# Decoder block: causal self-attention in six units of 512 score columns per row instead of eight

## What is computed

```python
def _L0_attn_ref(hidden_states, Wq, Wk, Wv, Wo):      # H=32, HKV=8, HD=16, S=128
    q = (hidden_states @ Wq.T).reshape(B, Sq, H, HD).transpose(0, 2, 1, 3)
    ...
    k = jnp.repeat(k, rep, axis=1)
    qr = apply_rope(q, cos, sin)
    kr = apply_rope(k, cos, sin)
    ...
    mask = jnp.where(causal_future[None, None, :, :], neg, mask)
    scores = jnp.einsum('bhqd,bhkd->bhqk', qr, kr) / np.sqrt(HD).astype(np.float32) + mask
    attn = jax.nn.softmax(scores, axis=-1)
    out = jnp.einsum('bhqk,bhkd->bhqd', attn, v)
    return out.transpose(0, 2, 1, 3).reshape(B, Sq, Dm) @ Wo.T
...
    x = x + _L0_attn_ref(_layernorm(x, axis=-1), ...)
    x = x + _L0_xattn_ref(_layernorm(x, axis=-1), ctx_4096, ...)
    x = x + _L0_ffn_ref(_layernorm(x, axis=-1), ...)
```

## Time and profile before

| | us |
|---|---|
| median of 3 runs | 1021.59 |
| lowest and highest | 1020.73, 1023.36 |
| the profiled execution | 1023.87 |
| its span | 1021.9 |
| TensorE busy | 951.2 (93%) |
| VectorE busy | 767.4 (75%) |
| ScalarE busy | 607.0 (59%) |
| GpSimd busy | 579.7 (57%) |

### The profile page before, as it was taken

The page is one execution under the profiler, slowest core; times in us unless marked ns, Lnnn a source line. Parts: engine busy times, 40 slices in busy tenths (PEclk is TensorE's granted clock), DMA queues, the critical chain, the costliest instruction groups (busy, mean ns, idle before and its releaser), DMA issues.

```text
span 1021.9 us, 17975 instructions
## 1 busy us (share of the span) xinstructions
PE 951.2 (93%) x5523; PEld 810.7 (79%) x5540; DVE 767.4 (75%) x1603; ACT 607.0 (59%) x2218; POOL 579.7 (57%) x586
## 2 busy tenths in 40 slices
PE   5888888876999999999999999999999999999977
PEld 4666666654888888888888888888888888888766
DVE  5788888775577777777777777777777777788965
ACT  1566666652585576567566755765676666656531
POOL 4443333203486568557656856765685676558743
PEclk9799999987999999999999999999999999999999
DMA  5000002000666646655665665556566555654531
GB/s 196 12 11 11 10 10 72 11 1 0 216 215 211 211 154 226 211 172 165 209 204 175 206 215 170 177 192 217 171 207 204 176 176 191 198 178 149 162 111 54
DMA packets 101138, 149.71 MB, mean 147 GB/s; under 512 B 11840, under 2 KB 77376, under 8 KB 98880
## 3 DMA queue, kind: packets, MB, share of 16 engines
q1 hardware_dynamic: 101056, 148.71, 45.8%
HBM read 87.85 MB, written 60.82 MB: 145 GB/s over the span
## 4 chain that ended last, share of the span: by engine, by line
PE 67%; DVE 4%; ACT 1%; POOL 1%; issue 1%; DMA 1%; SPq 0%; DVEq 0%; POOLq 0%
PE ps_kv L76 17%; PE ps_y L76 17%; PE ps_q L76 16%; PE ps_o L76 8%; PE ps_s L76 8%; ACT ps_s L1034 1%; DVE p L1146 1%; PE ps_f L76 1%; DVE neg_max L1134 1%; POOL pT_raw L952 0%; DVE p_blocks L1150 0%; DVE raw_wkv L1213 0%; DMA out<-raw_wq 0%; DVE kT_lo L1173 0%; DVE f_stats L1203 0%
## 5 line engine op out<-in xcount | busy, mean ns | idle before, releaser
L1034 ACT ACTIVATE ps_s<-ps_s,bias,q_rms 128x256 f32<-128x256 f32 x256 | 136.9, 535 | 139.6 <-DVE bias L1138 139.6
L945 POOL TENSOR_TENSOR qT_lo<-qk_raw,qT_hi 128x512 fp32r<-128x512 f32 x64 | 84.5, 1320 | 202.8 <-ACT qT_hi L1063 202.8
L952 POOL TENSOR_TENSOR pT_raw<-pT_raw,pT_hi_sb 128x1024 fp32r<-128x1024 f32 x64 | 154.4, 2412 | 11.8 <-ACT pT_hi_sb L1057 11.5
L1051 ACT ACTIVATE q_squares<-ps_q 128x128 bf16<-128x128 f32 x256 | 67.4, 278 | 112.1 <-DVE qk_blocks L1168 112.1
L76 PE MATMUL ps_y<-wo_hi,oT_hi 128*128 128x512 f32 x256 | 101.7, 397 | 4.9 <-DVE oT_lo L1184 4.9
L76 PE MATMUL ps_q<-wq_lo,xT_hi 128*128 128x512 f32 x256 | 101.4, 396 | 0.0
L76 PE MATMUL ps_q<-wq_hi,xT_lo 128*128 128x512 f32 x256 | 101.1, 395 | 0.0
L76 PE MATMUL ps_y<-wo_lo,oT_hi 128*128 128x512 f32 x256 | 101.1, 395 | 0.0
L1150 DVE STREAM_TRANSPOSE p_blocks<-p 128x512 f32<-128x512 f32 x128 | 91.1, 711 | 13.3
L76 PE MATMUL ps_q<-wq_hi,xT_hi 128*128 128x512 f32 x256 | 100.9, 394 | 0.0
L76 PE MATMUL ps_y<-wo_hi,oT_lo 128*128 128x512 f32 x256 | 100.9, 394 | 0.0
(11 more groups left out here) (205 smaller groups left out, 3027.6 us busy)
## 6 DMA issues: line engine op xcount, KB each, us to landing
p_scratch<-p_blocks SPq DMA_DIRECT2D x64, 512.0 KB, 3.0
pT_raw<-p_scratch SPq DMA_DIRECT2D x256, 128.0 KB, 3.0
qk_scratch<-qk_blocks SPq DMA_DIRECT2D x64, 384.0 KB, 3.5
qk_raw<-qk_scratch SPq DMA_DIRECT2D x256, 96.0 KB, 3.0
raw_wq<-in_x_wq SPq DMA_DIRECT2D x8, 1024.0 KB, 6.9
raw_wo<-in_x_wo SPq DMA_DIRECT2D x8, 1024.0 KB, 7.2
raw_wkv<-in_x_wkv SPq DMA_DIRECT2D x8, 512.0 KB, 5.0
ctx_raw<-in_ctxT SPq DMA_DIRECT2D x8, 256.0 KB, 2.5
```

The source lines that it names most:

```text
L945: pool.tensor_tensor(qT[1][:].rearrange("p g (i c) -> p g i c", i=4), qk_raw[s % 2][:, :, 0:XG, :].rearrange("p i g c -> p g i c"), f32(qT ...
L952: pool.tensor_tensor(raw, f32(raw), f32(pT_hi_sb[:].rearrange("p i t x -> p (i t x)")), ALU.subtract).then_inc(pT_lo, 1)
L1034: e = act.activation(scores, scores, ACT.Exp, bias=bias[:, g:g + 1], scale=q_rms[:, s % 4, g:g + 1], accum_out=total[:, g:g + 1])
L1051: i = act.activation(q_squares[:, g, :], ps_q[:, g * XD:(g + 1) * XD], ACT.Square, scale=XD ** -0.5, accum_out=q_mean[:, g:g + 1])
```

## The change

The fully masked quarter is not computed any more. The query positions are cut into a lower and an upper half of E = 64. For a lower half only the first 64 keys are taken. The transposes of the queries write the halves apart (halves_apart), so that a partition of a score tile no longer stands for one position of one head: an *upper* unit holds the upper halves of eight heads against all 128 keys, a *lower* unit the lower halves of sixteen heads against 64 keys. A unit is still 128 x 512 numbers. Per row there are four upper units (k = 0, 1, 3, 4) and two lower ones (k = 2, 5).

- scores: an upper unit has two float32r matmuls of 256 columns and a mask matmul of 256 columns; a lower one four float32r matmuls of 128 columns and a mask matmul of 512. The mask comes last.
- maxima: four maxima of 128 columns in an upper unit, eight of 64 in a lower one. exps: four exponentials of 128 columns, or eight of 64. That is 32 per row, as before.
- values: per half of the heads, four matmuls of 256 columns on groups of 32 array columns and two of 256 on groups of 64, with a second copy v_low of the values.
- k_stack is half as large and gives one key tile. ScalarE copies one half of it, VectorE the other behind it. kT, v_pad and v_low are held twice, by row parity. pad_values reads PSUM itself, in three copies.
- The mask is made on GpSimd from three selections and an addition in float32 (before: one selection in bfloat16). More memory is cleared at the start.
- The queues' orders are written anew, all eight rows as straight code with constant waits. At the start, the statistics of rows 2 to 7 and rope_keys(1) stand ahead of the first row's queries_low and maxima. The cross-attention's first weights are fetched one row earlier (row 5).
- The weights are laid out for the new order of heads outside the kernel.

```diff
+    E = S // 2
+    UNITS, UNITS_PER_HALF = 6, 3
+    LOWER = (2, 5)
+    TILE = (0, 1, None, 2, 3, None)
...
+        def total_columns(k):
+
+            h = k // UNITS_PER_HALF
+            if k in LOWER:
+                return [G * (4 * c + 2 * r + h) + 2 * m for c in range(2) for m in range(2) for r in range(2)]
+            return [G * (4 * (TILE[k] % 2) + 2 * r + h) + 2 * m + 1 for m in range(2) for r in range(2)]
+
+        def halves_apart(tile, at):
+
+            return tile[:].rearrange("p (m u a q) -> p m a u q", m=2, u=2, a=2)[:, at // 2, at % 2]
...
+            for m in range(1, B + 2):
+                if m < B:
+                    rotate_keys(m)
+                if m <= B:
+                    context(m - 1)
+                if m < B:
+                    rotate_queries(m)
+                if m == 1:
...
+            def exps(n, k):
+                act.wait_ge(max_ok, UNITS * n + k + 1)
+                wait(act, pT_ps, UNITS * n + k - 1)
+                if k == 0:
                     wait(act, inv_ok, n)
-                at = G * (2 * (j % 4) + j // 4)
-                for g in range(G):
-                    e = act.activation(p[:, j % 2, g, :], ps_s[j % 2][:, g * S:(g + 1) * S], ACT.Exp,
-                                       bias=neg_max[:, j % 2, g:g + 1], accum_out=total[:, at + g:at + g + 1])
+                width = E if k in LOWER else S
+                for t, at in enumerate(total_columns(k)):
+                    e = act.activation(p[:, k % 2, t * width:(t + 1) * width], ps_s[k % 2][:, t * width:(t + 1) * width], ACT.Exp,
+                                       bias=neg_max[:, k % 2, t:t + 1], accum_out=total[:, at:at + 1])
                 e.then_inc(exp_done, 1)
...
+            for n in range(-1, B + 1):
+                now, after = 0 <= n < B, n + 1 < B
+                if after:
+                    queries_high(n + 1)
+                if now:
+                    exps(n, 3)
+                if n + 2 < B:
+                    xn_high(n + 2)
+                if now:
+                    exps(n, 4)
+                if after:
+                    query_tiles(n + 1, 0)
+                    key_tiles(n + 1)
+                if now:
+                    exps(n, 5)
+                if after:
+                    query_tiles(n + 1, 1)
+                    query_tiles(n + 1, 2)
+                if n >= 1:
+                    x2_high(n - 1)
+                if now:
+                    inverse_transposed(n)
+                if after:
+                    exps(n + 1, 0)
+                if now:
+                    output_high(n)
+                if after:
+                    exps(n + 1, 1)
+                    query_tiles(n + 1, 3)
+                    exps(n + 1, 2)
...
+            def pad_values(m):
+                if m < 2:
+                    dve.wait_ge(zeroed, 9)
+                wait(dve, pv_ps, 2 * m - 2)
+                rows = ps_w[:, KVH * HD:2 * KVH * HD].rearrange("p (h c r d) -> p h c r d", h=2, c=2, r=2)
+                spread = v_pad[m % 2][:].rearrange("p (h w) -> p h w", h=2)[:, :, 0:P].rearrange("p h (t w) -> p h t w", t=4)
+                dve.tensor_copy(spread[:, :, :, 0:HD], rows.rearrange("p h c r d -> p h (c r) d"))
+                for r in range(2):
+                    spread = v_low[m % 2][E * r:E * r + E].rearrange("p (h w) -> p h w", h=2)[:, :, 0:P].rearrange(
+                        "p h (c r w) -> p h c r w", c=2, r=2)
+                    i = dve.tensor_copy(spread[:, :, :, r, 0:HD], rows[0:E, :, :, r, :])
+                i.then_inc(v_ok, 1)
...
+            def key_tiles(m):
+
+                dve.wait_ge(kT_ps, m + 1)
+                dve.wait_ge(kT1_sb, m + 1)
+                dve.tensor_copy(kT[m % 2][0:E, :, 0, :], ps_w[0:E, :].rearrange("p (h s) -> p h s", s=S)).then_inc(kT0_sb, 1)
...
+            for n in range(-1, B + 1):
+                now, after, later = 0 <= n < B, n + 1 < B, n + 2 < B
+                if after:
+                    rope_queries(n + 1)
+                if n == -1:
+                    rope_keys(0)
+                    pad_values(0)
+                    dve.wait_ge(x_in, 16)
+                    statistics(range(2, B))
+                    dve.wait_ge(stats_ok, B)
+                    for b in range(2, B):
+                        i = dve.bn_aggr(moments[:, b, :], stats[:, b, :])
+                    i.then_inc(moments_ok, 1)
+                if now:
+                    maxima(n, 3)
+                    probs_transposed(n, 0)
+                    probs_transposed(n, 1)
+                if later and n >= 0:
+                    normalised(n + 2)
+                if n >= 1:
+                    residual(n - 1)
+                if now:
+                    maxima(n, 4)
+                if after:
+                    queries_low(n + 1)
+                if now:
+                    probs_transposed(n, 2)
+                if after:
+                    key_tiles(n + 1)
+                if now:
+                    maxima(n, 5)
+                if later:
+                    xn_low(n + 2)
+                if n >= 1:
+                    statistics_2(n - 1)
+                if now:
+                    probs_transposed(n, 3)
+                    probs_transposed(n, 4)
+                if n >= 1:
+                    normalised_2(n - 1)
+                if n == B - 2:
+                    cross_weights_high(0)
+                if n == B - 1:
+                    cross_weights_high(1)
+                if now:
+                    inverse_totals(n)
+                    probs_transposed(n, 5)
+                if later:
+                    rope_keys(n + 2)
+                if after:
+                    maxima(n + 1, 0)
+                if n >= 1:
+                    x2_low(n - 1)
+                if now:
+                    output(n)
+                if after:
+                    maxima(n + 1, 1)
+                if later:
+                    pad_values(n + 2)
+                if now:
+                    output_low(n)
+                if after:
+                    maxima(n + 1, 2)
...
+            def key_tiles(m):
+                pe.wait_ge(k_lo, m + 1)
+                pe.wait_ge(v_ok, m + 1)
+                wait(pe, acc_ok, m - 1)
+                for h in range(4):
+                    pair = k_stack[:, 2 * h:2 * h + 2].rearrange("p r b a d -> p (r b a d)")
+                    mm = pe.transpose(ps_w[:, h * S:(h + 1) * S], f32(pair), ident[:])
+                mm.then_inc(kT_ps, 1)
...
+            def scores(n, k):
+
+                pe.wait_ge(qT_sb, 4 * n + (1, 2, 2, 3, 4, 4)[k])
+                pe.wait_ge(kT0_sb, n + 1)
+                pe.wait_ge(kT1_sb, n + 1)
+                wait(pe, exp_done, UNITS * n + k - 1)
+                tile, keys = ps_s[k % 2], kT[n % 2]
+                if k in LOWER:
+                    h = k // UNITS_PER_HALF
+                    for c in range(2):
+                        for m in range(2):
+                            at = (2 * c + m) * S
+                            pe.matmul(tile[:, at:at + S].rearrange("p (r s) -> p r s", r=2), qT[:, 2 * h + c, m, 0],
+                                      keys[:, 2 * h + c, :, 0:E], start=at == 0, stop=False)
+                    mm = pe.matmul(tile[:], ident16[:], mask[:].rearrange("p t s -> p (t s)"), start=False, stop=True)
                 else:
-                    pe.wait_ge(kT_sb, 2 * m + 1)
-                for h in range(4):
-                    mm = pe.transpose(ps_w[:, h * S:(h + 1) * S],
-                                      f32(k_stack[:, 4 * i + h].rearrange("p a b d -> p (a b d)")), ident[:])
-                mm.then_inc(kT_ps, 1)
-
-            def scores(n, j):
-                pe.wait_ge(qT_sb, 4 * n + j // 2 + 1)
-                pe.wait_ge(kT_sb, 2 * n + j // 4 + 1)
-                wait(pe, exp_done, KVH * n + j - 1)
-                tile = ps_s[j % 2]
-                pe.matmul(tile[:], ident16[:], mask[:].rearrange("p g s -> p (g s)"), start=True, stop=False)
-                for h in range(2):
-                    mm = pe.matmul(tile[:, 2 * h * S:(2 * h + 2) * S], qT[:, 2 * j + h, :],
-                                   kT[:, j].rearrange("p r s -> p (r s)"), start=False, stop=h == 1)
+                    for m in range(2):
+                        pe.matmul(tile[:, 2 * m * S:(2 * m + 2) * S], qT[:, TILE[k], m, 1],
+                                  keys[:, TILE[k]].rearrange("p r s -> p (r s)"), start=m == 0, stop=False)
+                    mm = pe.matmul(tile[:].rearrange("p (t s) -> p t s", t=4)[:, :, E:], ident16[:], mask[:, 0:4, :],
+                                   start=False, stop=True)
                 mm.then_inc(s_ps, 1)
...
+            for n in range(-1, B):
+                now, after, later = 0 <= n < B, n + 1 < B, n + 2 < B
+                if n >= 1:
+                    project_output(n - 1)
+                if now:
+                    scores(n, 4)
+                if later and n >= 0:
```

(38 more changed lines are left out.)

454 lines of the change are left out of this document (163 added, 291 removed).

## The result

| | before | after |
|---|---|---|
| median | 1022.48 (4 runs) | 992.32 (4 runs, 991.05 to 993.57) |
| the profiled execution | 1023.87 | 991.05 |
| its span | 1021.9 | 989.3 |

The ratio is 0.9696, with a 95% interval of 0.9669 to 0.9722: 30 us less. The forecast was 985 in a range of 975 to 1003, that is 37 less. The kernel before was timed once more beside the kernel after, at 1027.93, which moves its median from the 1021.59 shown ahead to 1022.48.

What follows compares the result with a forecast made beforehand. A ring of in-order queues bounds self-attention, TensorE and VectorE fullest at 86%. Terms 37.3 + 1.5 + 6 x 20.4 + 20.2 + 20.3 = 201.7 against 240.6, 38.9 less, with 2 allowed for slips 37 less: 985, range 975 to 1003.

Steps and rivals of the forecast that it cites:

- time 0: Start of project_queries(n+1), from which a row's steps are counted; for row 0 predicted at 37.3 us.
- the low clock: At the start, project_queries(1) was to run at a reduced TensorE clock, adding 1.5 us.
- allowance for slips: Over all rows, small waits the step-by-step timing rounds away: 0.25 us a row, 2 in all.
- The walk of a steady row: Step-by-step timing of each queue through one row in the new order: 20.4 us where it took 25.4.
- the knot: Around the keys' copies: VectorE idle 1.9 us, ScalarE idle from 13.3 to 14.9, TensorE waiting from 13.9 to 15.45.
- its rivals on prices: Lower units' scores cheap, 7 us less, 978 (20%); or 64-column exponentials costing as much as wide, 7 more, 992 (10%).
- the dear end: TensorE, lower unit's scores: 128-column matmuls at plain float32 rate, 0.22 us each, 1.1 with the mask; taken for the forecast.
- the cheap one: TensorE, lower unit's scores: 128-column matmuls never dearer than 256-column ones, 0.13 us, 0.6 with mask; 978 in all (20%).
- The rival of dear narrow exponentials: ScalarE: 64-column exponentials cost as much as 128-column ones, 0.42 twice a row, 7 us more, 992 (10%).
- The gaps stay: Every row still stands 3.6 us above its fullest engine: 22.8 us a row, 17 longer in all, 1002 (22%).
- the slower rival: VectorE and GpSimd collide in four VectorE operations of each row: 6.5 us more, a row of 26.9, 1030 (3%).
- none of the four runs then: Normalised, queries_low, normalised_2 and inverse_totals on VectorE were to miss GpSimd's rotations and context split in each row.

Runs made afterwards that it cites:

- the straight kernel before: The kernel before with its loop over rows 1 to 5 written out as straight code with constant waits; median 1019.77, ratio 0.9969.
- the first run with all edits: Kernel after: weight splits moved off rows' rotations, statistics of rows 2 to 7 behind queries_low(0), VectorE's key copy not waiting for ScalarE's; 963.46, ratio 0.9438.

## Why the prediction was right, point by point

The sum against the profile, each from time 0 as the prediction counts it:

| | predicted | measured |
|---|---|---|
| time 0 of row 0 | 37.3 | 36.4 |
| row 0 | 21.9 (20.4, and 1.5 for the low clock) | 23.9 |
| rows 1 to 5 | 5 x 20.4 | 100.2 |
| row 6 | 20.2 | 24.4 |
| row 7 | 20.3 | 21.4 |
| allowance for slips | 2 | none seen |
| the unedited rest | 781.3 | 783.05 |

That sums to 985.0 of span, and with 2.0 between span and execution it is the 987 forecast for the profiled kind. Measured are 991.05: collisions 7.3 more (2.0, 4.2, 1.1), the rest of the kernel 1.8 more, steady rows 1.8, time 0 0.9 and the allowance 2 less. The number is near in part by luck, because these partly cancel.

*The rows.* The walk of a steady row held. query tile 1 was to come at 15.45 after time 0 and came at 14.80; exps(n, 5) at 14.9, came at 14.1; from query tile 1 to the end of the row 4.95, measured 5.18. Most of the difference ahead of the knot is the lower units' scores, below. The knot's three gaps were to be 1.9, 1.6 and 1.5 and were 1.57, 1.42 and 1.20. That one wait makes them is shown: without it the row is 18.58. The prediction priced the knot's gaps but not the wait itself, which is worth more (8.8 us between the profiled executions) than either of its rivals on prices (7).

*TensorE's price of a lower unit.* This step was wrong: the dear end, 1.1, was taken for want of a row, and the cheap one was right. Four matmuls of 128 columns and the mask take 0.70, or 0.63 for unit 2 (103.39 to query tile 3 at 104.02). The choice by the nearest row (plain float32 of the values) missed that those are 32 columns of the array wide and another type; which of the two makes them slower, no run shows. The Trainium skill (TensorEngine Tiling (Array Packing), Instruction Overhead) has a floor of about 60 cycles for a matmul and names no other penalty. The trace agrees in that none shows at 128 columns (0.12 each), though they are no cheaper than those of 256 columns (0.11 to 0.13) either. The values took 1.15 for 1.00, well inside the 0.4 allowed for their two groupings.

*ScalarE's price* of 64 columns, 0.29, held at 0.29 to 0.30. The rival of dear narrow exponentials is out.

*VectorE.* Busy 17.75 for 17.4: output_low takes 1.45 in place of 0.69, beside GpSimd's context split (122.53 beside 122.14 in the next row). The Trainium skill (GPSIMD Engine Reference, Specifications) has contention for operations with two SBUF inputs, and the trace agrees. It costs the row nothing, since the maxima behind it wait for scores anyway.

*The start.* exps(0,0) was to come at 37.6 and came at 37.47; queries_low(0) was to start at 27.2 and started at 27.42. The loss of 5.5 against the earlier trace rows is as large as forecast. Of its two causes the statistics are not shown to be the larger: with them behind queries_low, exps(0,0) comes 20.0 behind the end of the cast in place of 20.4, and with them behind xn_low and no wait in the knot 17.9 to 18.0, while the straight kernel before has 14.9. One term did not come at all: project_queries(1) was to lose 1.5 to the low clock and took 2.88 (36.37 to 39.25), as in a steady row. That the clears on GpSimd cost nothing was not right in general: they are part of what VectorE's cast waits for. Before, the cast took 4.89 too, so the difference of the two profiles has none of it.

*The gaps stay* (1002) is out: a steady row is 1.3 above its fullest engine, not 3.6.

*Collisions.* The mechanism of the slower rival was there, but in three rows only. The step that failed is "none of the four runs then": it went through GpSimd's rotations and context split, and left its weight splits out, of wo in row 0 (4.60) and of the cross-attention's in rows 6 and 7 (2.34, 4.50). In the steady rows the statement held. The text ahead of the prediction names the cross-attention's splits, and its quote of the new order has their high halves on VectorE; wo's split stands in the code at the place where the quote of GpSimd's queue ends (`if m == 1:`). For the last one the walk took its length as time on GpSimd, and not as time for which VectorE stands beside it. Against the walk rows 0, 6 and 7 cost 7.3 us more. Taking the splits out of the way brought 13 to 14. The two differ because the walk had paid for part of it: 1.5 in row 0 for a low clock that did not come, in row 7 the same for project_output(6) (5.16 in the walk, 2.84 in the trace, 189.11 to 191.95), and behind it cross-attention's wait for the low half of wq, which the early split ends.

## What to carry to other kernels

When work is cut out of a ring of in-order queues, price the cut by the order too: here the cut units were worth 1.8 us of a row and the rest of the rewrite, mostly its order, 2.95, and one needless wait between two readers of one PSUM tile held back another 1.4. Lay GpSimd's long operations on SBUF against VectorE's queue one by one, the rare ones (weights, clears) above all, and place them where VectorE only works from PSUM or has nothing on the path. If a row's busy time of VectorE grows without more work, look for an operation that ends with one of GpSimd's.

## What the runs showed of the hardware

*VectorE can stand for the whole of an unbroken row of GpSimd's operations.* A widening of 0.43 took 4.56 beside one split of 4.50. normalised(0), 0.55, took 3.16 beside six clears that followed each other without a gap, in both kernels with the clears first. The first half of wq's cast takes 0.69; the second took 4.9 to 5.8 beside the split of wkv and two to six clears behind it, and 2.87 where VectorE came in between the split and the clears. The Trainium skill (SBUF — State Buffer, SBUF: two separate sides) describes the port that the two share as a lock held for one whole instruction, on which the other blocks. The single collisions fit that; the six clears go beyond it, as VectorE did not get in between them. Casts that started at 10.90 and 10.91 took 5.77 and 2.87 in two kernels with the same start of both queues (the one without the wait in the knot and the one with wo early, the split beside them at 10.55 and 10.56): what decides it was not found, and it moves all that follows by 3 us.

*What isn't held up.* Six statistics took 3.64 to 3.66 both beside GpSimd's split of wo and without it, and copies out of PSUM keep their 0.68. wq's second subtraction, of two SBUF inputs, kept its 1.22 beside the clears, in the first run with all edits (VectorE, then GpSimd):

```profile
13.90 1.22 DVE L502 TENSOR_TENSOR wq_lo<-raw_wq,wq_hi 128x1024 fp32r<-128x1024 f32 x1
```
```profile
13.26 2.39 POOL L225 MEMSET a_kT<- 128x1024 f32 x2
```

output_low, also of two SBUF inputs, doubled beside a subtraction. The same section of the Trainium skill has such operations contend only against one of GpSimd that reads SBUF, and this agrees.

*Fast float32 matmuls of 128 columns* cost what those of 256 do, no more and no less: four take 0.48 us up to the start of the mask (110.17 to 110.65), 0.12 each, and those of 256 columns in project_keys_values start 0.11 to 0.13 apart.
